# A gated cross-attention and mixture-of-experts layer: output projection and second norm's statistics one step later in each attention body

## The reference, cut to what matters

```python
x = x + tanh(g_xattn) * xattn(layernorm(x), ctx, ctx, Wq, bq, Wk, bk, Wv, bv, Wo, bo)   # 16 heads of 16, softmax over 256 keys
x = x + tanh(g_ffn) * moe(layernorm(x), Wr, br, W1, b1, W2, b2)                         # 8 experts, top 2, hidden 1024, relu
```

## Time and profile before

| what | value |
|---|---|
| median of 3 runs | 836.75 us (835.48 to 837.84) |
| the profiled execution, its own time | 833.6 us |
| its span, first to last instruction | 831.8 us |
| mean granted TensorE clock | 0.963 of full speed |
| busy, share of the span | PE 87%, PEld 59%, DVE 73%, ACT 49%, POOL 55% |
| attention bodies | from about 24 us to 400 us |
| expert stage | from about 430 us to the end |

### The profile page before, as it was taken

One profiled execution on the slowest core, in us unless ns is written; L12 is line 12 of the kernel. 1 busy time (PEld: TensorE's weight loads), 2 busy tenths in 40 slices (PEclk: granted clock), 3 DMA queues, 4 the chain that ended last, 5 costly groups with the idle time before them and its releaser, 6 DMA issues.

```text
span 831.8 us, 21356 instructions
## 1 busy us (share of the span) xinstructions
PE 726.9 (87%) x6536; PEld 488.2 (59%) x6537; DVE 609.4 (73%) x1256; ACT 406.4 (49%) x783; POOL 458.8 (55%) x453
## 2 busy tenths in 40 slices
PE   2679999888888888877879999999999999999982
PEld 2335555454555544433657777777777777777761
DVE  5668888889898889996356787667666666676653
ACT  2256777677776767675333333333333333333330
POOL 6224444566565676437447677755655555556522
PEclk9689999999999999997689999999999999999997
DMA  6436656676767665553312232343232222333321
GB/s 188 121 85 207 187 162 183 164 191 173 187 154 172 185 183 162 155 141 114 69 49 46 40 52 46 52 54 52 46 48 46 44 48 46 50 50 49 44 32 20
DMA packets 96790, 85.32 MB, mean 103 GB/s; under 512 B 22257, under 2 KB 86001, under 8 KB 96593
## 3 DMA queue, kind: packets, MB, share of 16 engines
q1 hardware_dynamic: 80752, 65.73, 29.1%
q0 software_dynamic: 15680, 18.69, 14.2%
q10 hardware_dynamic: 288, 0.00, 0.0%
HBM read 53.61 MB, written 30.62 MB: 101 GB/s over the span
## 4 chain that ended last, share of the span: by engine, by line
PE 41%; DVE 19%; issue 16%; DMA 9%; POOL 8%; ACT 4%; POOLq 1%; DVEq 0%; ACTq 0%; SPq 0%
PE banks L1765 10%; DMA out_dram<-yb,dest_idx 7%; DVE negmax L1119 7%; PE banks L1661 5%; POOL xg L704 4%; PE banks L1747 4%; PE banks L1749 4%; PE banks L1748 4%; PE banks L1577 3%; ACT probs L931 2%; PE banks L1649 2%; PE banks L1563 2%; POOL out_dram L778 2%; DVE stats L1043 2%; PE banks L1702 2%
## 5 line engine op out<-in xcount | busy, mean ns | idle before, releaser
L994 ACT ACTIVATE hid<-banks,b_col 128x256 f32<-128x256 f32 (+1 forms) x312 | 124.2, 452 | 219.3 <-PE banks L1749 112.9
L1765 PE MATMUL banks<-wall,hh 128*128 x568 | 204.8, 380 | 1.4 <-DVE hl L1458 1.0
L778 POOL DMA_INDIRECT out_dram<-yb,dest_idx x71 | 124.8, 1757 | 126.8 <-DMA out_dram<-yb,dest_idx 58.5
L1119 DVE TENSOR_REDUCE negmax<-banks 128x4 f32<-128x1024 f32 x128 | 155.7, 1217 | 20.7 <-PE banks L1628 20.0
L1747 PE MATMUL banks<-xh,wall 128*128 128x256 f16 (+1 forms) x624 | 163.2, 266 | 5.2 <-ACT hid L994 4.3
L931 ACT ACTIVATE probs<-banks 128x1024 f32<-128x1024 f32 x128 | 131.1, 1024 | 71.8 <-PE banks L1649 70.8
L1749 PE MATMUL banks<-xh,wall 128*128 128x256 f16 (+1 forms) x624 | 163.2, 266 | 0.0
L1748 PE MATMUL banks<-xl,wall 128*128 128x256 f16 (+1 forms) x624 | 163.2, 266 | 0.0
L1765 PE MATMUL banks<-wall,hl 128*128 x568 | 144.3, 273 | 0.0
L1661 PE MATMUL banks<-probs,vaug 128*32 128x256 f32 x1024 | 84.4, 402 | 26.1 <-ACT probs L931 15.3
L689 POOL DMA_INDIRECT token_lists<-entry,place_i x64 | 69.2, 1082 | 66.4 <-ACT probs L931 41.9
(11 more groups left out here) (203 smaller groups left out, 1177.6 us busy)
## 6 DMA issues: line engine op xcount, KB each, us to landing
raw<-in_L_ffn_W SPq DMA_DIRECT2D x16, 512.0 KB, 5.7
wst<-in_L_ffn_W SPq DMA_DIRECT2D x16, 512.0 KB, 6.4
k_parts<-kparts SPq DMA_DIRECT2D x48, 128.0 KB, 5.5
q_parts<-qparts SPq DMA_DIRECT2D x48, 128.0 KB
ks<-k_parts SPq DMA_DIRECT2D x64, 96.0 KB, 2.3
qs<-q_parts SPq DMA_DIRECT2D x64, 96.0 KB, 2.2
xin<-in_x SPq DMA_DIRECT2D x16, 256.0 KB, 2.9
cin<-in_ctx SPq DMA_DIRECT2D x16, 256.0 KB, 3.3
```

What stands on the lines that cost most here:

```text
L778: nc.gpsimd.indirect_dma_start(out_rows, bass.IndirectOffsetOnAxis(dest_idx[par][:, s:s + 1], 0), yb[par][:, s, :], None, compute_op=ALU.a ...
L994: ins = nc.scalar.activation(hid[half][:, c % (HC // 2), 0:subs(j) * P], banks[:, b, c % 2 * TS:c % 2 * TS + subs(j) * P], ACT.Relu, bias= ...
L1119: nc.vector.tensor_reduce(negmax[:, c, 8 * (g // 2):8 * (g // 2) + 8].rearrange("p (m g p2) -> p m g p2", m=2, g=2)[:, :, g % 2, :], banks ...
L1765: ins = nc.tensor.matmul(dst, h_[:, c, s * P:(s + 1) * P], w_, start=(c == 0 and k == 0), stop=(c == HC - 1 and k == 1))
```

## The change

On VectorE, `attended_low` goes behind `reduce` in step 3, and `residual` and `norm2_stats` go from step 4 (before `reduce` of step 5) to step 5 (behind it, and behind the step's router instructions). On TensorE, the first half of `output` goes from step 3 to step 4 (still ahead of the turn of the maxima) and the second from step 4 to step 5, between `scores_max` and `v`. In bodies without maxima (16) and in the code behind the bodies the work is otherwise the same.

```diff
                     if w == 1 and ahead:
                         k_low(m + 1)
+                    if maxima:
+                        reduce(m, w)
                     if w == 3 and post:
                         attended_low(m - 2)
-                    if maxima:
-                        reduce(m, w)
...
                     elif w == 4 and post:
-                        residual(m - 2)
                         if listing:
                             top_numbers()
-                        norm2_stats(m - 2)
-                        if listing:
                             top_first()
                             top_onehot(1)
                             spacing(q)
                             pick(q)
+                    elif w == 5 and post:
+                        residual(m - 2)
+                        norm2_stats(m - 2)
...
                     elif u == 3:
                         if ahead:
                             q(m + 1, 1)
+                    elif u == 4:
                         if post:
                             output(m - 2, 0)
-                    elif u == 4:
-                        if post:
-                            output(m - 2, 1)
                         if maxima:
                             turn_max(m, 0)
                     elif u == 5:
+                        if post:
+                            output(m - 2, 1)
                         if maxima:
                             v(m, par, ahead)
```

## The result

| | kernel before | changed kernel |
|---|---|---|
| median | 837.07 us (835.48 to 837.84) | 886.12 us (884.67 to 887.54), 4 runs |
| ratio | 1 | 1.0589, 95% interval 1.0565 to 1.0612 |
| profiled execution, its span | 833.6, 831.8 us | 884.67, 882.9 us |
| mean granted TensorE clock | 0.963 | 0.92 |
| norm2 turn of the last item (15, in the code behind the bodies) | 426.21 us | 478.09 us |

The change costs 49 us, where 22 were forecast and the range ended at +29: right in sign, wrong in size by a factor of more than two. The last row says where: the last item has its norm2 turn 51.9 us later, and the span is 51.1 us longer, so everything is lost ahead of it, in the attention bodies, and the expert stage takes what it took.

The account below looks back on a forecast made before the run. Instruction order was taken as the bound, with GpSimd's chain within a microsecond of setting body ends. Later x1b and slowed xn2b summed to 24.0 us over the bodies, taken as +22: 855.6 profiled, 858.5 median; range 849 to 866.

Parts of the forecast that it names:

- Bound and direction: Attention bodies: instruction order bounds, GpSimd's chain nearly sets each end, removing TensorE's low-part wait gains nothing; slower, chance 0.93.
- Output one step later: TensorE, second output half before v: seventh attend 0.13 us later in even bodies, 0.67 in odd ones.
- x1b 2.0 us later, xn2b 3.1 and 3.5 us, then the turn and the keys: Body ends: x1b +2.1 even, +1.96 odd; xn2b lasts 3.1 and 3.5 us; bodies +2.2 and +2.1 us.
- The meeting of xn2b and the low part: GpSimd's xn2b beside VectorE's expert weights' low part: lasts 3.1 us (even) or 3.5 (odd) in place of 2.43.
- the upper sum: All attention bodies, with xn2b slowed by VectorE's low part: 24.0 us in total.
- the free one: All attention bodies, with xn2b at 2.43 us, unslowed by VectorE's low part: 13.7 us in total.
- the earlier trace: At 229.22 GpSimd began a normalization 0.06 us before such a VectorE instruction and needed 3.51 us, not 2.43.
- rival 4: Late GpSimd chain delays list entries; next body's xres and xn meet VectorE: 1 us more in 8 bodies, 867 us; chance 0.09.
- the peeled odd bodies' free case: Bodies 3, 5, 13 with xn2b unslowed by VectorE's low part: +0.7 us each.

Follow-up runs that it names:

- e4: Kernel before with the low part behind the maximum and both output halves in TensorE's step 4, residual in place; 837.55 us, ratio 1.001.
- e8: Kernel before, nothing moved, with GpSimd computing xn2b twice in a row; 885.13 us, ratio 1.0552.
- e2: Kernel before with only the residual and the statistics moved behind the maximum of VectorE's step 5; 885.28 us, ratio 1.0574.
- e1: Changed kernel with 16 filler matmuls on TensorE ahead of the wait for xn2b; 868.68 us, ratio 1.0373.
- e6: Changed kernel with fillers ahead of last attend (10), xn2b wait (16) and keys (8), and the expert weights' second low part in VectorE's step 7; 870.05 us.
- e11: e10 with VectorE's one-hot row and gate sum moved from step 2 to step 3; 861.7 us, ratio 1.0307.
- e10: Changed kernel with fillers ahead of the last attend (10) and the wait for xn2b (16), none ahead of the keys; 867.93 us, ratio 1.0377.

## Why the prediction was wrong in size

- **Bound and direction: right.** The wait on the low part was not on the path (e4: 6.5 us less of it, no gain), and GpSimd's chain set the ends of the bodies (e8: that chain alone made late gives the full loss).
- **Output one step later, +0.1 and +0.7 us a body: hidden, as the sum had it.** The sum went by x1b and didn't add this term. e2 without it and the changed kernel with it differ by less than e2's interval.
- **x1b 2.0 us later, xn2b 3.1 and 3.5 us, then the turn and the keys: right.** The ends of the bodies came out at 6.8 us for 6.7 and 7.0, and at full clock (e1) the loop's bodies 8, 9 and 10 at 26.2, 24.2 and 25.8 for 25.9 and 23.7.
- **The meeting of xn2b and the low part: there, its price open.** xn2b took 3.06 to 3.50 us in bodies 3 to 14. e1's nine bodies at full clock, with the meeting in them, fit the upper sum (18.6 us for 16.9) and not the free one (9.6); e6, which took the meeting away, brought another in and gained 2.3. On which engine gets the ports: in both bodies shown VectorE had begun first (289.61 before 290.08, 259.92 before 260.23) and GpSimd was held, which the rule of the Trainium skill (SBUF — State Buffer, "SBUF: two separate sides") gives as well as the earlier trace rows do, so these rows don't decide between them.
- **Clock: the step that failed.** The sum took each instruction at its duration in the kernel before and added only waits. It had no term and no rival for what a wait does to the matmuls behind it. What the runs show in its place: the keys behind the wait took 2.77 us for 1.47, the time at the lower level went from 27 to 109 us, and filling the wait with work took that to 41 us and the time down by 17.4. With the clock held up that far the change costs 868.7 - 836.3 = 32 us; with it falling, 49. So some 17 of the 27 us that were missing are the clock's.
- **The other 10 us: not separated.** e1's excess over the forecast stands almost wholly in the four bodies in which its clock still falls (15.8 us for 6.9), so part of it may be the clock's too. Against that, e6 with 17 us at the lower level was no faster than e1 with 41. The fillers are work of their own and shift what meets what, so no run shows the bare order at full clock.
- **Small instructions in step 2: named in rival 4, and not the cause.** Its price was a guess, and such meetings stood in the kernel's own trace; but they add up to nearly the same before and after the change (6.8 and 7.1 us). e11, which has none, is at +26 us; the kernel that it is compared with has them, so this may be too low for the cost of the order.
- **Slips in the working.** 833.6 + 22 + 3.15 is 858.75, not 858.5; the peeled odd bodies' free case is 1.9 - 1.35 = 0.55, not 0.7. Neither matters here.

So of the 49, 17 are shown to be the clock's and 32 are left for the order of the work, with whatever the clock still costs in e1, for a forecast of 22 to 24. The first was missing in the forecast; the second was worked out, and what it is short by stays open. Each share is good to a few microseconds.

## What to carry to other kernels

A new wait on TensorE has two prices: its own length, and nearly twice the time for the matmuls behind it if the clock falls (here 2.77 us for 1.47). Before adding a wait of a microsecond, read how busy TensorE is in the microseconds ahead of it; where it already has gaps, price the dense work behind the wait at both levels and give that case its own rival. And ask of a removed wait who is late next: here 6.5 us of it could go for nothing, while moving one producer a step down (e2) cost the full 49.

## What the runs showed of the hardware

- In body 4 of the changed kernel the clock went to 1.2 GHz in a wait of 1.1 us, behind three microseconds with 0.57, 0.62 and 0.48 of work, and stayed there for 6.8 us, in which the engine was nearly all the time busy. In the kernel before, microseconds with 0.76, 0.70 and 0.40 left it at 2.4 GHz, and so did 0.17, 1.00, 0.94 and 0.18.
- Sixteen small matmuls without use, 1.07 us of TensorE in a body, made the kernel 17.4 us faster. They are a mend of the symptom: the kernel with them is still 3.7% slower than the one before.
- A VectorE instruction on 128x4 elements with one input took 1.91 us beside a GpSimd list entry and tensor instruction, in place of 0.16, although it had begun 0.6 us ahead of the latter (e10). In body 11 of e1 such a meeting was followed by a wait of 1.52 us on TensorE and a fall of the clock.
